# Who takes the input layernorm's roots, who loads the stacks, and when rows are zeroed, in a graph attention and two-of-eight experts kernel

## The reference, cut to what matters

```python
# x: (8, 1024, 128) float32; adj: (1024, 1024) of 0 and 1
x = x + gnn(layernorm(x), adj, ...)
x = x + ffn(layernorm(x), ...)

def layernorm(x): return (x - mean(x)) / sqrt(var(x) + 1e-5)

def gnn(x, adj, ...):                       # x: (8, 1024, 128), 4 heads of 32
    q, k, v = x @ Wq.T + bq, x @ Wk.T + bk, x @ Wv.T + bv
    scores = clip(q @ k.T / sqrt(32), -10, 10)          # per head, 1024 x 1024
    scores = where(adj == 0, -10, scores)
    attn = softmax over each chunk of 128 keys           # 8 chunks
    out = (sum over chunks of attn @ v) @ Wo.T + bo + x
    return layernorm(out) * gamma + beta

def ffn(x, ...):                            # 8192 tokens, 8 experts, the best 2 of them
    out = sum over the 2 best experts of prob * (gelu(x @ W1[e] + b1[e]) @ W2[e] + b2[e])
```

## Time and profile before

| | us |
|---|---|
| median of 3 runs | 817.09 (816.98 to 817.26) |
| the profiled execution | 815.88 |
| its span | 814.1 |
| attention, first clip to last chunk of the last batch on GpSimd | 36.4 to 522.8 |
| one batch in the middle (batch 3 to batch 4, GpSimd's L593) | 55.2 |
| batch 1 to batch 2, the same row | 63.0 |

### The profile page before, as it was taken

One profiled execution on the slowest core, in us unless ns is written; L12 is line 12 of the kernel. 1 busy time (PEld: TensorE's weight loads), 2 busy tenths in 40 slices (PEclk: granted clock), 3 DMA queues, 4 the chain that ended last, 5 costly groups with the idle time before them and its releaser, 6 DMA issues.

```text
span 814.1 us, 20184 instructions
## 1 busy us (share of the span) xinstructions
PE 665.5 (82%) x6427; PEld 382.6 (47%) x6427; DVE 675.7 (83%) x1701; ACT 559.2 (69%) x1091; POOL 552.4 (68%) x567
## 2 busy tenths in 40 slices
PE   4598499999699999999999885685330699999994
PEld 1333134434234334334344232463220699999994
DVE  4989989989599899899899996786572498888893
ACT  4697397995797997988989865654300577777772
POOL 1210818787699899898998999867877155555554
PEclk9999899999899999999999998766555699999998
DMA  8826105446425326236154200401111222232210
GB/s 275 245 82 165 67 26 166 138 114 167 116 69 177 104 93 167 76 116 161 66 152 134 78 22 0 104 28 45 44 51 54 52 69 65 82 82 78 63 47 3
DMA packets 60700, 78.22 MB, mean 96 GB/s; under 512 B 8229, under 2 KB 33666, under 8 KB 60595
## 3 DMA queue, kind: packets, MB, share of 16 engines
q1 hardware_dynamic: 42962, 45.26, 18.4%
q10 hardware_dynamic: 12672, 23.07, 10.6%
q0 software_dynamic: 4960, 8.58, 3.3%
HBM read 56.05 MB, written 22.59 MB: 97 GB/s over the span
## 4 chain that ended last, share of the span: by engine, by line
PE 34%; ACT 18%; DVE 14%; POOL 13%; issue 8%; DMA 8%; ACTq 3%; SPq 1%; POOLq 0%; DVEq 0%
DMA qk_dram<-qk_lo 6%; POOL rows_dram L627 6%; ACT w L776 5%; PE score_ps L1558 4%; ACT prob_ring L776 4%; PE sum_ps L1572 4%; PE side_ps L1588 3%; ACT ctx_sb L756 3%; POOL ctx_sb L566 3%; PE score_ps L1516 3%; ACTq L742 3%; PE score_ps L1518 3%; PE score_ps L1517 3%; ACT xn L698 2%; PE sum_ps L1798 2%
## 5 line engine op out<-in xcount | busy, mean ns | idle before, releaser
L1007 DVE SCALAR_TENSOR_TENSOR prob_ring<-score_ps,limit 128x1024 f32<-128x1024 f32 x128 | 149.5, 1209 | 17.0 <-PE score_ps L1558 16.6
L776 ACT ACTIVATE prob_ring<-prob_ring 128x1024 f32<-128x1024 f32 x128 | 133.1, 1056 | 40.6 <-DVE prob_ring L1007 22.4
L1558 PE MATMUL score_ps<-stack_mem 128*128 128x512 f16 x512 | 140.3, 389 | 25.0 <-DVE prob_ring L1007 19.6
L1007 DVE SCALAR_TENSOR_TENSOR w<-score_ps,limit 128x1024 f32<-128x1024 f32 x128 | 149.9, 1214 | 8.7 <-PE score_ps L1558 8.4
L566 POOL TENSOR_TENSOR ctx_sb<-ctx_sb,rspread 128x512 f32<-128x512 f32 x108 | 139.2, 1289 | 23.6 <-POOL ctx_acc L571 9.5
L776 ACT ACTIVATE w<-w 128x1024 f32<-128x1024 f32 x128 | 134.1, 1055 | 28.7 <-issue 14.0
L634 POOL DMA_INDIRECT out_x<-xn,limit x91 | 90.3, 992 | 86.3 <-DVE xn L1395 71.1
L571 POOL TENSOR_TENSOR ctx_acc<-ctx_acc,ctx_sb 128x512 f32<-128x512 f32 x93 | 118.9, 1278 | 7.3
L901 ACT ACTIVATE xn<-score_ps,vec 128x128 f32<-128x128 f32 x364 | 99.4, 385 | 11.6 <-PE score_ps L1518 10.6
L1558 PEld LDWEIGHTS score_ps<-stack_mem 128*128 128x128 f16 x512 | 37.7, 98 | 125.1 <-issue 49.5
L627 POOL DMA_INDIRECT rows_dram<-x,limit x64 | 65.1, 1017 | 27.6 <-issue 19.0
(11 more groups left out here) (240 smaller groups left out, 1583.8 us busy)
## 6 DMA issues: line engine op xcount, KB each, us to landing
rspread<-rinv_dram SPq DMA_DIRECT2D x84, 256.0 KB
stack_mem<-qk_dram ACTq DMA_DIRECT2D x56, 256.0 KB, 4.7
ctx_sb<-rows_dram SPq DMA_DIRECT2D x91, 66.5 KB, 2.0
qk_dram<-qk_hi ACTq DMA_DIRECT2D x16, 256.0 KB, 2.8
qk_dram<-qk_lo ACTq DMA_DIRECT2D x16, 256.0 KB, 5.9
x<-in_adj SPq DMA_DIRECT2D x4, 512.0 KB, 7.6
ctx_sb<-in_adj SPq DMA_DIRECT2D x4, 512.0 KB, 10.0
stack_mem<-qk_dram SPq DMA_DIRECT2D x16, 128.0 KB, 3.2
```

The lines of the kernel that those rows point to most:

```text
L776: act.activation(prob_at(s, u), prob_at(s, u), ACT.Exp, scale=1.0 / SCORE).then_inc(exp_done, 1)
L1007: dve.scalar_tensor_tensor(out=prob_at(s, u), in0=score_ps[:, 2 * u:2 * u + 2, :], scalar=-LIMIT * SCORE, in1=limit[:, k:k + 1, half * HAL ...
L1558: ins = pe.matmul(score_ps[:, h, :], kstack[:, par, h, k * P:k * P + P], qstack[:, par, h, half * HALF:half * HALF + HALF], start=True, st ...
```

## The change

- The input layernorm's root for batches 1 to 7 goes to GpSimd: VectorE makes mean and variance with `bn_aggr` (8 instructions per batch, new `prep_moments`), GpSimd takes four instructions per span with its power operation (`prep_root`), and mean and root are kept in the rows of x1. Spans are now batch 1 (ahead of the first step), batches 2 and 3 (GpSimd step 5 of batch 0), batches 4 to 7 (GpSimd step 15 of batch 1). The statistics for batches 2 and 3 are made in steps 0 and 1 of batch 0, for 4 and 5 in steps 13 and 15, for 6 and 7 in steps 0 and 8 of batch 1.
- SyncE issues the stack loads of batches 1 to 7, between two groups of spreads.
- The 29 stores of zero rows go to the start of batch 0, behind the load of x.
- For batch 0, q's parts are stored after the third projection and k's after the fourth, with a semaphore for each; the stack loads wait for each apart.
- Four of the eight groups of the mask are turned and copied ahead of the first score, two more in step 0 and two in step 1. The raw mask lies in `prob_ring`, which clips first touch in step 2.
- In batch 0 the preparation of batch 1 stands one step later (transposes in steps 2 and 3, projections in 4 to 7, stores in 7 and 9), `prep_xn` is split over steps 1 and 2, and the small copies `copy_consts` and three of the bias go to step 9.

```diff
+            def prep_root(i):
+                rows = x1_rows(BATCHES[i].start, BATCHES[i].stop)
+                rstd, shift = rows[:, :, RSTD], rows[:, :, SHIFT]
+                pool.wait_ge(moments_ready, i)
+                pool.tensor_scalar(rstd, rstd, EPS, 1.0, ALU.add, ALU.mult).then_inc(prep_root_step, 1)
+                pool.tensor_scalar(shift, shift, -1.0, 1.0, ALU.mult, ALU.mult)
+                pool.wait_ge(prep_root_step, 2 * i - 1)
+                pool.tensor_tensor(rstd, rstd, neg_half[:, 0:1].to_broadcast([P, T * len(BATCHES[i])]), ALU.pow).then_inc(prep_root_step, 1)
+                pool.wait_ge(prep_root_step, 2 * i)
+                pool.tensor_tensor(shift, shift, rstd, ALU.mult).then_inc(shift_ready, 1)
...
+            for b in range(NB):
+                if b:
+                    load_spreads(2 * b - 1)
+                if b < LAST:
+                    stack_parts(b + 1, 0)
+                    stack_parts(b + 1, 1)
+                    load_spreads(2 * b)
...
+                    if first and EARLY + 2 * s < T:
+                        limit_copy(EARLY + 2 * s)
+                        limit_copy(EARLY + 2 * s + 1)
...
+                    if s == 15 and second:
+                        prep_root(3)
...
-                    if first and s in (9, 10, 11, 13):
-                        i = (9, 10, 11, 13).index(s)
-                        prep_stats(2, BATCHES[2][i:i + 1])
-                    if first and s == 14:
-                        prep_rsqrt(2)
+                    if first and s in (0, 1):
+                        prep_stats(2, BATCHES[2][s:s + 1])
+                    if first and s in (2, 3):
+                        prep_moments(2, BATCHES[2][s - 2:s - 1])
+                    if first and s == 9:
+                        bias_parts()
+                        copy_consts()
+                    if first and s in (13, 15):
+                        prep_stats(3, BATCHES[3][s // 15:s // 15 + 1])
+                    if second and s in (0, 8):
+                        prep_stats(3, BATCHES[3][2 + s // 8:3 + s // 8])
+                    if second and s in (1, 7, 10, 13):
+                        prep_moments(3, BATCHES[3][(1, 7, 10, 13).index(s):(1, 7, 10, 13).index(s) + 1])
```

163 lines of the change are left out of this document (91 added, 72 removed).

## The result

The changed kernel takes **794.32 us** (792.31 to 796.59), the one before beside it 817.17 (816.98 to 818.19): ratio 0.9719, 95% interval 0.9691 to 0.9746. The forecast was 794.4. The profiled execution took 792.31 with a span of 790.5, against 815.88 and 814.1 before.

The account below looks back on a forecast made before the run. VectorE and ScalarE bound until the second group's first chunk, then GpSimd's list; 13.5 us gained by batch 1's post_final, less 6.3 for the root, plus 11.5 and 5.0, is 23.7, less 1 friction: 817.1 - 22.7 = 794.4, range 789.5 to 803.

Parts of the forecast that it names:

- The start: Ahead of batch 0's first step: first clip 2.9 us sooner, eaten by ScalarE's mask copies; 0.3 us behind by step 9.
- Batch 0 to batch 1, step 3: VectorE's gapless stretch from step 9, root and statistics removed; 13.3 us gained by the second group's first chunk, start included.
- the floor of 2.83 us: Shortest step, set by TensorE's scores; steps 11 and 14 of batch 0 fall to it, 0.8 us lost.
- The first chunk of the second group: GpSimd's row where the path passes from VectorE and ScalarE to GpSimd; at 104 us, 117.36 before.
- `post_final` at 141.1: First half of batch 1's post_final on GpSimd comes 13.5 us sooner: 13.3 - 1.8 + 2.0.
- The 2.0 us for ScalarE's wait: GpSimd's wait of 2.04 us for ScalarE in batch 1, step 14, goes, since ScalarE no longer stands in step 8.
- The root of 5.5 us: Power operation on 32 columns on GpSimd in batch 1, step 15: 5.5 us, 6.3 with its neighbours, on the path.
- Batch 2: With zero rows moved, GpSimd's waits of 5.6 + 0.9 for spreads and 5.0 ahead of post_final go: 11.5 us.
- Later waits, 5.0: GpSimd's remaining waits ahead of post_final go with ScalarE's stall in steps 8 and 10: 5.0 us.
- Friction of 1 us: 1 us given back for waits between three engines that now run at the same rate: 23.7 becomes 22.7.
- A lost lead: Rival: GpSimd doesn't keep its lead, waits ahead of post_final stay, 801.7; 0.23 together with zero rows hindering batch 0.
- The other rivals: Power operation not growing beyond 8 columns, 790.5, chance 0.1; next batch's stack landing late behind spreads, about 824, chance 0.03.

Follow-up runs that it names:

- e5: Changed kernel plus one spare power operation on 32 columns on GpSimd, step 8 of batch 3, and a small memset ahead of the attention: 800.74 us.
- e6: Changed kernel plus eight spare statistics instructions on VectorE in step 12 of each of batches 3, 4 and 5: 797.23 us.
- e1: Changed kernel with the 29 stores of zero rows put back behind the third group of spreads, in batch 2: 801.8 us.
- e2: Changed kernel with the stack loads of batches 1 to 7 issued by ScalarE again: 799.34 us.
- e3: Changed kernel with the root of batches 4 to 7 back on VectorE, behind step 14 of batch 0, its statistics in steps 8, 10, 11, 13: 806.37 us.
- e8: Changed kernel with GpSimd's root of batches 4 to 7 in step 10 of batch 0, statistics and moments made earlier in batch 0: 792.2 us.
- e9: Changed kernel with the root of batches 4 to 7 ahead of GpSimd's first post_root of batch 1, moments taken sooner: 788.53 us.
- e11: The changed kernel measured once more, with no edit: 795.22 us.
- e7: The kernel before the change with only the 29 stores of zero rows moved to the start of batch 0: 809.8 us.

## Why the prediction was right, point by point

- **The path.** Right: VectorE up to the first groups, GpSimd's list from there (e5, e6).
- **The start.** The first clip at 33.55 for the 33.5 said; over the nine profiled executions of kernels that differ only behind it (after, e1, e2, e3, e5, e6, e8, e9, e11; e5 has a memset more) it is 32.75 to 35.82. By step 9 I had put it 0.3 us behind; it was 66.29 for 64.96 before, 1.3 behind. And this is the early end: in e1, e2, e5, e6, e9 and e11, with no edit to the work of these steps, step 9 stands at 66.35 to 70.70, 1.4 to 5.7 behind, with more of the first steps at half clock in the late ones. The sum has no term for the clock; this is its largest gap.
- **Batch 0 to batch 1, step 3.** 100.56 for 113.63 before, 13.1 for the 13.3 said. From step 9 on it is 14.4 for the 13.6 in the sum, which makes up for most of the miss at the start. Of the 0.8 that I took off for the floor of 2.83 us little shows: step 14 took 2.26, as it did before without its root. The root on VectorE and its companions were the large part (e3).
- **The first chunk of the second group.** Said 104, was 105.51. It wasn't VectorE that was late: GpSimd was still in the first eight chunks, released by its own L589, since their first spread had come late. Timeline of SyncE and GpSimd after:

```profile
66.61 10.00 SPq L445 DMA_DIRECT2D stack_mem<-qk_dram  x8
76.65 0.43 SPq L451 DMA_DIRECT2D rinv_dram<-prob_ring  x1
81.89 8.36 SPq L458 DMA_DIRECT2D rspread<-rinv_dram  x6
...
88.09 1.28 POOL L584 TENSOR_TENSOR ctx_sb<-ctx_sb,rspread 128x512 f32<-128x512 f32 x1 [5.86 <-DMA rspread<-rinv_dram]
```

  The store of the reciprocals stands behind the eight stack loads in SyncE's list, of whose 10.0 us some 6 are a wait for k's parts to land: a wait that the change added and that I had priced only for the stack, not for the spreads. It cost nothing, because GpSimd then waited 5.55 us for the moments.
- **`post_final` at 141.1.** It came at 141.10. The lag of 1.5 us at the first chunk was gone by then, and the wait for the moments that the prediction named was there. That it is right to a hundredth is luck, since e11 has 145.45. The 2.0 us for ScalarE's wait were 1.7 (0.32 left of 2.04), but the stack loads are not the cause of most of it: given back to ScalarE in e2 they bring back 0.6.
- **The root of 5.5 us.** 5.48 on 32 columns, 2.94 on 16, and 6.45 with its neighbours for the 6.3 said. That is what it adds to GpSimd's list; taken off the list again it gives only 4.7, because 1.76 us of other waits then come up (e9).
- **Batch 2.** I had 11.5 us for the zero rows and the wait of 5.0, and period 1 to 2 was to be 5.2 shorter. It was 4.5 shorter. GpSimd's busy time in it rose from 48.45 to 54.64 us, 6.2 for the root's 6.3, and its idle time fell from 14.5 to 3.9, 10.7 for the 11.5: both terms nearly right. But the 11.5 are not the zero rows' alone, which have 7.5 (e7); the rest went with the other parts, 1.8 of it hidden behind the root (e9). With root and zero rows both out of the way the period is 53.82 (e9). ScalarE's wait for the ring was 1.93 for "some 3".
- **Later waits, 5.0.** 4.8 (1.0 in period 2 to 3, 3.8 in 3 to 6). The period is 54.4, GpSimd's own list. The number is right, its cause only in part: the sum gave all of it to ScalarE's stall, and e2, which has the stall again, loses 2.6 of the 4.8. The other 2.2 no run isolates; e7, with neither root nor stack loads moved, has none of the 4.8 (55.43 and 167.8).
- **Zero rows between 33 and 52.** Issued from 33.16 to 55.80, 22.64 us for 29, with the DMA engines at 0.71 of their time in 50 to 54 us; nothing waited for them (e1, and e7 gains what e1 loses).
- **Friction of 1 us, and the rivals.** The sum said 23.7 at the end of the attention, 22.8 was there. The 1 us of friction was no wait that the trace shows: it stands for the terms above that came out 0.9 short together. A lost lead would show as idle time ahead of `post_final`: none from batch 2 on. The other rivals fell with the rows on the power operation and with a stack that was never late (its last loads landed 8 to 14 us ahead of the next batch's first clip, and TensorE waited for none).
- **From the profiled execution to the median.** The two executions differ by 23.6 us, the medians by 22.9: the profiled execution of after is the shortest of its four. That the forecast of 794.4 meets the median of 794.32 to a tenth is luck: the same kernel had 795.22 in e11, single executions spread over 4 us, and the sum left out a start that varies by as much.

## What to carry to other kernels

Follow one instruction that recurs once per stage on the engine that sets the end, and compare its starts: a delay ahead of it, one in a period and one behind it are then told apart, even where whole runs of the same program differ by 4 us. Work that must go to the engine that bounds goes where that engine waits anyway, and its price on the path is its length less the waits that it swallows there, which adding or moving it alone shows. When a load moves to another engine's queue, price everything queued behind it, not only who waits for the load. And when a term comes out right, undo its part alone: here undoing brought back 0.6 of 1.7 us in one place and 2.6 of 4.8 in the other.
